# Last attention layer of a four-layer graph network: the weighted sum of values taken tile by tile with fp32 probabilities as the held operand, in place of fp16 halves summed over pairs of tiles

## Chip, cores, metric

One core of one Trainium2 chip. The metric is the device time of one execution in microseconds (us), median of the runs shown. TensorE does the matmuls, VectorE (DVE) and ScalarE (ACT) the work on rows, GpSimd (POOL) constants and some reductions, SyncE (SP) issues the transfers.

## What is computed

Four graph layers over 1250 nodes with 512 features, each behind a layer norm and a ReLU and each added to x. The change touches only the last one, cut here to what it computes:

```python
def _L3_gnn_ref(x, batch, ei, W):        # x is relu(layernorm(x)) of 1250 x 512
    scaling = float(64) ** (-0.5)
    q, k, v = jnp.split(x @ W, [512, 1024], axis=-1)
    q = (q * scaling).reshape(n, 8, 64)
    k = k.reshape(n, 8, 64)
    v = v.reshape(n, 8, 64)
    aw = jnp.einsum('ehf,ehf->eh', q[src], k[dest])
    m = jax.ops.segment_max(aw, src, num_segments=n)
    e = jnp.exp(aw - m[src])
    denom = jax.ops.segment_sum(e, src, num_segments=n)
    alpha = e / denom[src]
    out = jax.ops.segment_sum(alpha[:, :, None] * v[dest], src, num_segments=n)
    return out.reshape(n, 512)
```

There are 20000 edges, 8 heads of 64 features. The kernel holds the edges as a dense 1250 x 1250 table of counts, so a repeated edge is a count above one, and its logarithm is added to the score.

## The kernel before, in words

The nodes are 10 tiles of 125 rows. Per engine there is one hand-written program (`block.tensor`, `block.scalar`, `block.vector`, `block.sync`, `block.gpsimd`); the order of the work on an engine is the order in which its loops issue it, and semaphores tie the engines together. `after(eng, name, n)` is a wait for a count.

**Values.** In the last layer, per tile of nodes, TensorE makes v in 12 fp16 matmuls of 512 columns (L1826) into `psW[t % 2]`. ACT (L822) writes the upper half of v, scaled, as fp16 into `v_pair[.., t, h, 0, :]`; DVE (L1323) writes v minus that half as fp16 into `v_pair[.., t, h, 1, :]`. Around these stand, on the same two engines, the norm of a later tile (L802), the upper and lower halves of the turned h (L808, L1310) and of the weights (L632, L1250). `project_half` then makes k and q (L62), and `projected_up` and `projected_low` split these (L829, L1331).

**The loop.** Then 80 steps of a pipeline follow, one for each head h and tile t of targets (n = 10h + t). On TensorE step n issues, in this order: `turn_tile(n-2)`, 10 fp32 transposes (L1385) of the 125 x 1250 row of probabilities into `psW[1]`; a first part of the weighted sum; `score(n+1)`, 6 fp16 matmuls (L62) into `psW[0]`; the rest of the weighted sum; and in every second step `fold_pair`.

- DVE adds the logarithm of the counts to the scores and takes the row maximum (L1368), makes the negative maximum (L1371), and later, per four tiles, `add_quad` (L1352, L1353, L1358) divides and adds the four results to x.
- ACT takes the exponential with its row sum (L856), into `row3[n % 3]`.
- The turned probabilities (source on the partitions, target along the free dimension) leave PSUM twice: ACT (`upper`, L841 for blocks 0 to 7 and L843 for blocks 8 and 9) writes fp16 upper halves of 2^15 times the value, DVE (`lower`, L1344, L1346) the fp16 rest. `turned_a` and `turned_b` are these two pieces of `psW[1]`. The next tile's transposes wait for DVE's pieces (`lo3a`, `lo3b`).
- `weigh_pair` (L1879) works on two tiles of targets at once, spread over two steps (5 blocks in each, as 3 and 2 round the score): per block of 125 sources it holds v's two halves side by side (125 x 128 fp16) and streams first the two tiles' upper halves, then their lower halves (250 columns each), all 20 into one 128 x 250 result. ACT copies that result to `o_sum` (L545, 128 x 250). `fold_pair` (L1892) turns it back per tile and adds the two halves of v with a constant 128 x 64 matrix `fold`, made by POOL at the start.

```python
for j in blocks:
    for part in range(2):
        m = pe.matmul(small[:, 0:2 * ROWS], v_pair[0:ROWS, j, h, :, :].rearrange("p c d -> p (c d)"),
                      turned[pair % 2][0:ROWS, j, 2 * part:2 * part + 2, :].rearrange("p c i -> p (c i)"), ...)
```

## Time and profile before

| | us |
|---|---|
| median of 3 runs | 1238.27 |
| lowest, highest | 1237.48, 1239.95 |
| the profiled execution, its own time | 1239.9 |
| span of the profiled execution | 1238.2 |
| TensorE matmul busy in the span | 1132.0 |
| VectorE busy | 914.5 |
| ScalarE busy | 716.0 |

The trace lists weight loads (PEld) and matmuls (PE) of TensorE apart; the two overlap, and matmuls are pipelined, so the recorded duration of one matmul is longer than the distance to the next. The distance from one load to the next, or from one group's first load to the next group's first, is what a group of matmuls takes out of TensorE's time. A fp32 matmul that is no transpose is two records in the trace, a load and a matmul each. The last layer's loop of 80 steps runs from about 913 us to 1232 us of the span; the values are made from 832 us to 865 us. PEclk is the granted clock of TensorE as a share of the full one.

### The profile page before, as it was taken

The page shows a single profiled execution, that of the slowest core. Times are in us where ns is not written, and L with a number is a line of the kernel's source. Part 1 is how long each engine was busy: PE and PEld are TensorE (multiplying, and loading weights), DVE is VectorE, ACT ScalarE, POOL GpSimd, SP SyncE. Part 2 cuts the span into 40 slices and gives each one's busy share as a digit, 9 for nine tenths or more (in the row PEclk, how much of TensorE's full clock was granted, in tenths as well). Part 3 has the DMA queues.
Part 4 walks back from the last instruction along what each step waited for, and adds up shares of the span by engine and source line. Part 5 has one row for each costly group of instructions (what it writes and reads, how often), then busy time and mean ns, then how long its engine had stood idle before and what let it go on. Part 6 is the DMA issues. An engine that isn't in the chain of part 4 may idle for free. (4 is left out here: it accounts for less than half of the span.)

```text
span 1238.2 us, 16225 instructions
## 1 busy us (share of the span) xinstructions
PE 1132.0 (91%) x5959; PEld 714.8 (58%) x5959; DVE 914.5 (74%) x1652; ACT 716.0 (58%) x901; POOL 64.5 (5%) x117
## 2 busy tenths in 40 slices
PE   6999969996999977979999999969999999999996
PEld 4666635555785544434444444436557777777775
DVE  5999962017656697878899997865448888888885
ACT  2324846005548666058877877845137777777774
POOL 3000132000002100000000000000000000000000
PEclk9899989998999987979999999989999999999999
DMA  4000000003003000204111100000021001111002
GB/s 157 5 1 1 1 2 2 1 0 136 1 1 95 1 1 1 85 24 147 45 45 44 45 24 2 2 1 1 1 52 27 20 8 27 27 27 27 2 1 83
DMA packets 24771, 36.18 MB, mean 29 GB/s; under 512 B 11874, under 2 KB 13204, under 8 KB 24694
## 3 DMA queue, kind: packets, MB, share of 16 engines
q1 hardware_dynamic: 24694, 35.14, 9.4%
q8 instruction: 50, 0.82, 0.3%
q14 instruction: 27, 0.22, 0.1%
HBM read 26.03 MB, written 2.70 MB: 23 GB/s over the span
## 5 line engine op out<-in xcount | busy, mean ns | idle before, releaser
L62 PE MATMUL wide<-arena 125*125 125x512 bf16 (+5 forms) x2076 | 462.2, 372 | 16.3 <-DVE arena L962 7.5
L62 PEld LDWEIGHTS wide<-arena 125*125 125x125 bf16 (+5 forms) x2076 | 253.9, 131 | 197.9 <-issue 80.7
L1783 PE MATMUL wide<-arena 125*65 125x512 f32 (+1 forms) x480 | 182.3, 516 | 0.0
L1385 PE MATMUL wide<-ident,arena 125*125 125x125 f32 (+3 forms) x954 | 132.0, 286 | 11.6 <-ACT arena L618 4.2
L758 ACT ACTIVATE arena<-arena,b 125x1250 f32<-125x1250 f32 x80 | 106.7, 1336 | 60.1 <-PE wide L1783 55.8
L1278 DVE TENSOR_TENSOR arena<-wide,arena 125x1250 f32<-125x1250 f32 x80 | 116.7, 1459 | 31.2 <-PE wide L1773 31.1
L1385 PEld LDWEIGHTS wide<-ident,arena 125*125 125x125 f32 (+3 forms) x954 | 116.5, 187 | 21.8 <-issue 8.9
L841 ACT ACTIVATE arena<-wide 125x1000 f16<-125x1000 f32 x80 | 80.8, 1010 | 79.7 <-PE wide L1385 79.7
L1783 PEld LDWEIGHTS wide<-arena 125*65 125x65 f32 x480 | 63.4, 138 | 101.8 <-issue 95.4
L1344 DVE SCALAR_TENSOR_TENSOR arena<-wide,arena 125x1000 f16<-125x1000 f32 x80 | 95.9, 1199 | 33.6 <-ACT arena L841 33.6
L856 ACT ACTIVATE arena<-arena,neg_max,unit 125x1250 f32<-125x1250 f32 x80 | 114.3, 1429 | 5.7 <-DVE neg_max L1371 5.7
L1219 DVE CUSTOM_DVE_ANT_0 arena<-arena,cnt 125x1250 bf16<-125x1250 f32 x80 | 116.2, 1452 | 1.5 <-DVE b_max L1219 1.5
L1879 PE MATMUL small<-arena 125*128 125x250 f16 x800 | 112.7, 271 | 1.4 <-DVE arena L1346 1.4
L790 ACT ACTIVATE arena<-arena,b 125x1250 f32<-125x1250 f32 x80 | 106.0, 1325 | 8.4 <-DVE arena L1278 8.4
L961 DVE TENSOR_SCALAR arena<-arena 125x1250 bf16<-125x1250 f16 x180 | 98.4, 546 | 8.2 <-issue 7.3
L1385 PE MATMUL small<-ident,arena 125*125 125x125 f32 (+6 forms) x360 | 61.6, 314 | 44.3 <-ACT arena L575 15.3
L545 ACT ACTIVATE arena<-cntT 125x1250 f16<-125x1250 int16 x64 | 75.7, 1235 | 25.7 <-PE wide L62 25.4
L1879 PEld LDWEIGHTS small<-arena 125*128 125x128 f16 x800 | 72.1, 98 | 27.8 <-issue 20.2
L1385 PEld LDWEIGHTS small<-ident,arena 125*125 125x125 f32 (+6 forms) x360 | 52.9, 208 | 52.7 <-issue 18.6
L545 ACT ACTIVATE arena<-wide 65x512 f32<-65x512 f32 (+4 forms) x50 | 29.9, 640 | 76.4 <-PE wide L1453 50.1
L1771 PE MATMUL wide<-arena,sel_w 128*125 128x512 bf16 (+1 forms) x240 | 59.4, 357 | 15.5 <-DVE arena L1278 12.1
L990 DVE BATCH_NORM_STATS2 bns<-arena 128x6 f32<-128x512 f32 (+1 forms) x36 | 18.7, 581 | 62.7 <-ACT arena L673 62.6
(255 smaller groups left out, 1260.1 us busy)
## 6 DMA issues: line engine op xcount, KB each, us to landing
arena<-rows_kept SPq DMA_DIRECT2D x16, 625.0 KB, 5.9
arena<-arena SPq DMA_DIRECT2D x40, 156.2 KB, 2.9
arena<-in_L_gnn_W SPq DMA_DIRECT2D x3, 1024.0 KB, 7.7
x_nm<-in_x SPq DMA_DIRECT2D x2, 1250.0 KB
out<-x_nm SPq DMA_DIRECT2D x1, 2187.5 KB
arena<-in_L_gnn_W_l SPq DMA_DIRECT2D x1, 1024.0 KB, 6.3
arena<-in_L_gnn_W_r SPq DMA_DIRECT2D x1, 1024.0 KB, 8.4
arena<-in_L_gnn_Wk SPq DMA_DIRECT2D x1, 1024.0 KB, 5.3
```

Of the source, the lines that this page charges most:

```text
L62: mm = pe.matmul(ps[0:rows, lo:hi], lhsT, rhs[:, lo:hi], start=start, stop=stop, skip_group_check=True)
L545: return act.activation(dst, src, ACT.Copy, **k)
L758: act.activation(ring[n % RINGS][0:ROWS, :], t_bc[h % 2][0:ROWS, :], ACT.Relu, scale=0.8, bias=b08[0:ROWS, h, t:t + 1]).then_inc(S["relu2_ ...
L790: act.activation(row, row, ACT.Exp, bias=b02[0:ROWS, h, t:t + 1]).then_inc(S["exp2_made"], 1)
L856: act.activation(row, row, ACT.Exp, bias=neg_max[0:ROWS, n % TILES:n % TILES + 1], scale=unit[0:ROWS, 0:1], accum_out=den3[0:ROWS, n:n + 1 ...
L961: ts(hot_src[0:ROWS, g, :], iota_h[0:ROWS, :], e_col[0:ROWS, 1, c + g, :], None, ALU.is_equal)
L1219: dve.tensor_tensor_reduce(junk[0:ROWS, :], b_bc[h % 2][0:ROWS, :], mask[0:ROWS, i, :], 1.0, 2 * NEG, ALU.subtract, ALU.max, b_max[0:ROWS, ...
L1278: tt(row, psW[0][0:ROWS, 0:N], row, ALU.add).then_inc(S["z2_made"], 1)
L1344: stt(wide(2 + s), turned_a, UP, wide(s), ALU.mult, ALU.subtract).then_inc(S["lo3a"], 1)
L1385: return pe.transpose(dst, src, ident[0:k, 0:k])
L1783: m = pe.matmul(psW[1][0:VA, lo:hi], v_gat[0:ROWS, t, h, :], ring[n % RINGS][0:ROWS, lo:hi], start=(t == 0), stop=(t == TILES - 1))
L1879: m = pe.matmul(small[:, 0:2 * ROWS], v_pair[0:ROWS, j, h, :, :].rearrange("p c d -> p (c d)"), turned[pair % 2][0:ROWS, j, 2 * part:2 * p ...
```

## The change

The probabilities stay fp32. `turned` is now four buffers of 125 x 1250 fp32, one for each tile. ACT copies blocks 0 to 7 (`turned_out`), DVE blocks 8 and 9 (`turned_rest`), with no second pass and no factor 2^15. v is kept as fp32 `v_last`, written by DVE alone. `weigh(n, blocks)` holds a block of turned probabilities (125 sources x 125 targets, fp32) and streams v of that block (64 columns, fp32), so that the result of 10 matmuls is already the 125 x 64 of one tile, in the place in `small` where `add_quad` reads. `fold`, `o_sum`, `weigh_pair` and `fold_pair` are gone; the weighted sum runs three steps behind the score's step, 6 blocks ahead of the score and 4 behind it.

```diff
-        v_pair = region(16384, [TILES, H, 2, DH], F16)
+        v_last = region(16384, [TILES, H, DH])
-        o_sum = [region(13870 + 250 * i, [2 * ROWS]) for i in range(2)]
-        turned = [region(5120 + 2500 * i, [TILES, 4, ROWS], F16) for i in range(2)]
+        turned = [region(5120 + 1250 * i, [TILES, ROWS]) for i in range(QUAD)]
...
-            done(pool.memset(fold[:, :], 0.0))
-            for r in range(2):
-                done(pool.affine_select(out=fold[:, :], in_=fold[:, :], compare_op=ALU.not_equal, fill=1.0, base=-r * DH,
-                                        pattern=[[-1, DH]], channel_multiplier=1))
...
-                    act.wait_ge(S["v3_full"], t + 1)
-                    act.activation(v_pair[0:ROWS, t, :, 0, :], psW[t % 2][0:ROWS, 0:512].rearrange("p (h d) -> p h d", h=H), ACT.Copy,
-                                   scale=SCALED).then_inc(S["v3_hi"], 1)
...
+                def turned_out(n):
+
                     act.wait_ge(S["turned3a"], n + 1)
-                    if s == 0:
-                        after(act, "pv3_full", pair - 1)
-                    act.mul(dst[:, 0:8, :].rearrange("p (b c) i -> p b c i", b=2), turned_a, UP).then_inc(S["hi3a"], 1)
-                    act.wait_ge(S["turned3b"], n + 1)
-                    act.mul(dst[:, 8:10, :], turned_b, UP).then_inc(S["hi3b"], 1)
-
-                for n in range(H * TILES + 5):
-                    if n >= 6 and n % 2 == 0:
-                        pair = (n - 6) // 2
-                        act.wait_ge(S["pv3_full"], pair + 1)
-                        after(act, "folded3", pair - 1)
-                        copy(o_sum[pair % 2], small[:, 0:2 * ROWS]).then_inc(S["o3_out"], 1)
-                    if 2 <= n < H * TILES + 2:
-                        upper(n - 2)
+                    after(act, "pv3_full", n - QUAD + 1)
+                    copy(turned[n % QUAD][0:ROWS, 0:8, :].rearrange("p (b c) i -> p b c i", b=2), turned_a).then_inc(S["turned3a_out"], 1)
+
+                for n in range(H * TILES + 2):
+                    if n >= 2:
+                        turned_out(n - 2)
...
-                    dve.wait_ge(S["v3_hi"], t + 1)
-                    stt(v_pair[0:ROWS, t, :, 1, :], psW[t % 2][0:ROWS, 0:512].rearrange("p (h d) -> p h d", h=H), SCALED,
-                        v_pair[0:ROWS, t, :, 0, :], ALU.mult, ALU.subtract).then_inc(S["v3_out"], 1)
+                    dve.wait_ge(S["v3_full"], t + 1)
+                    ts(v_last[0:ROWS, t, :, :], psW[t % 2][0:ROWS, 0:512].rearrange("p (h d) -> p h d", h=H), SCALED, None,
+                       ALU.mult).then_inc(S["v3_out"], 1)
...
+                def turned_rest(n):
+
+                    dve.wait_ge(S["turned3b"], n + 1)
+                    after(dve, "pv3_full", n - QUAD + 1)
+                    dve.tensor_copy(turned[n % QUAD][0:ROWS, 8:10, :], turned_b).then_inc(S["turned3b_out"], 1)
...
-                    if n >= 9 and (n - 9) % QUAD == 0 and (n - 9) // QUAD < H * TILES // QUAD - 1:
-                        add_quad((n - 9) // QUAD)
-                    if 2 <= n < H * TILES + 2:
-                        lower(n - 2)
+                    if n >= 8 and n % QUAD == 0 and n // QUAD - 2 < H * TILES // QUAD - 1:
+                        add_quad(n // QUAD - 2)
+                    if n >= 2:
+                        turned_rest(n - 2)
...
+                def weigh(n, blocks):
+
+                    q, h = n // QUAD, n // TILES
                     if blocks[0] == 0:
-                        pe.wait_ge(S["lo3b"], 2 * pair + 2)
-                        after(pe, "o3_out", pair)
+                        pe.wait_ge(S["turned3a_out"], n + 1)
+                        after(pe, "acc_read", H + q - 1 if q >= 2 else 0)
+                    at = 512 * (q % 2) + DH * (n % QUAD)
                     for j in blocks:
-                        for part in range(2):
-                            m = pe.matmul(small[:, 0:2 * ROWS], v_pair[0:ROWS, j, h, :, :].rearrange("p c d -> p (c d)"),
-                                          turned[pair % 2][0:ROWS, j, 2 * part:2 * part + 2, :].rearrange("p c i -> p (c i)"),
-                                          start=(j == 0 and part == 0), stop=(j == TILES - 1 and part == 1))
+                        if j == 8:
+                            pe.wait_ge(S["turned3b_out"], n + 1)
+                        m = pe.matmul(small[0:ROWS, at:at + DH], turned[n % QUAD][0:ROWS, j, :], v_last[0:ROWS, j, h, :],
+                                      start=(j == 0), stop=(j == TILES - 1))
...
-                for n in range(H * TILES + 5):
+                for n in range(H * TILES + 3):
...
+                    if n >= 3:
+                        weigh(n - 3, range(6))
                     if n + 1 < H * TILES:
                         score(n + 1)
-                    if 4 <= n < H * TILES + 4:
-                        weigh_pair((n - 4) // 2, (range(5 * half + 3, 5 * half + 5)))
-                    if n >= 6 and n % 2 == 0:
-                        fold_pair((n - 6) // 2)
+                    if n >= 3:
+                        weigh(n - 3, range(6, TILES))
```

TensorE's own order in one step of the loop, before (out<-in, rows x columns; L1892 the fold, L1385 the transposes, L1879 the weighted sum, L62 the score):

```order
L1892 MATMUL small<-fold,arena 125x64 [waits acc_read,o3_out]
L1892 MATMUL small<-fold,arena 125x64
L1385 MATMUL wide<-ident,arena 125x125 [waits lo3a,exp3_made]
L1385 MATMUL wide<-ident,arena 125x125 x7
L1385 MATMUL wide<-ident,arena 125x125 [waits lo3b]
L1385 MATMUL wide<-ident,arena 125x125
L1879 MATMUL small<-arena 128x250 x6
L62 MATMUL wide<-arena 125x512 [waits score3_read]
```

And now (L1361 the transposes, L1857 the weighted sum, L61 the score):

```order
L1361 MATMUL wide<-ident,arena 125x125 [waits turned3a_out,exp3_made]
L1361 MATMUL wide<-ident,arena 125x125 x7
L1361 MATMUL wide<-ident,arena 125x125 [waits turned3b_out]
L1361 MATMUL wide<-ident,arena 125x125
L1857 MATMUL small<-arena 125x64 [waits acc_read,turned3a_out]
L1857 MATMUL small<-arena 125x64 x5
L61 MATMUL wide<-arena 125x512 [waits score3_read]
```

The fold is gone; the six matmuls ahead of the score hold 125 targets and stream 64 columns where they streamed 250; the transposes wait for a copy by ACT where they waited for DVE's second half.

DVE's order in one step, before (L1368 the sum with its maximum, L1344 and L1346 the lower halves):

```order
L1368 ISA arena,mcol<-wide,cnt 125x1250 [waits score3_full,turned3b]
L1368 ISA mcol 125x1
L1371 TENSOR_SCALAR neg_max<-mcol,unit 125x1 [waits score3_read]
L1352 TENSOR_SCALAR den<-den,unit 125x4 [waits folded3]
L1353 RECIPROCAL den<-den 125x4 [waits dve_done]
L1358 SCALAR_TENSOR_TENSOR x_nm<-small,den,x_nm 125x64 [waits dve_done]
L1358 SCALAR_TENSOR_TENSOR x_nm<-small,den,x_nm 125x64 x3
L1344 SCALAR_TENSOR_TENSOR arena<-wide,arena 125x8x125 [waits hi3a]
L1346 SCALAR_TENSOR_TENSOR arena<-wide,arena 125x2x125 [waits hi3b]
```

And now:

```order
L1344 ISA arena,mcol<-wide,cntT 125x1250 [waits score3_full,turned3b]
L1344 ISA mcol 125x1
L1347 TENSOR_SCALAR neg_max<-mcol,unit 125x1 [waits score3_read]
L1328 TENSOR_SCALAR den<-den,unit 125x4 [waits pv3_full]
L1329 RECIPROCAL den<-den 125x4 [waits dve_done]
L1334 SCALAR_TENSOR_TENSOR x_nm<-small,den,x_nm 125x64 [waits dve_done]
L1334 SCALAR_TENSOR_TENSOR x_nm<-small,den,x_nm 125x64 x3
L1322 COPY arena<-wide 125x250 [waits pv3_full,turned3b]
```

The pass over 125 x 8 x 125 behind the four-tile sum has left DVE; a copy of 125 x 250 remains.

## Rows read from the trace of the kernel before

**Rows 1.** The page's busy line, and the loop by windows (busy us, PEclk, DMA)

```profile
PE 1132.0 (91%) x5959; PEld 714.8 (58%) x5959; DVE 914.5 (74%) x1652; ACT 716.0 (58%) x901; POOL 64.5 (5%) x117
...
945.00:1222.00 277.00, 272.38 (x2030) 210.44 (x2029) 243.74 (x469) 205.53 (x328) 0.00 (x0) 1.00 0.10 23
```

**Rows 2.** The chain of waits from 900 us on: shares by line, two recurring pieces

```profile
by line: PE wide L1385 27.1%; PE wide L62 26.8%; PE small L1879 20.7%; ACT arena L856 7.5%; PE small L1892 4.5%; issue 3.9%; ACT arena L841 3.0%; ACT arena L843 2.0%; DVE arena L1344 1.4%; DVE arena L1368 0.4%; DVE arena L1331 0.4%; DVE x_n
...
951.29 1.41 ACT arena L856 x2
...
1195.83 1.41 ACT arena L856 x2
```

**Rows 3.** Timeline of TensorE's loads in one step: start, us, engine, line, operation

```profile
1002.10 0.52 PEld L1892 LDWEIGHTS small<-fold,arena 128*125 128x125 f32 x4
1002.53 1.17 PEld L1385 LDWEIGHTS wide<-ident,arena 125*125 125x125 f32 x10
1003.62 0.64 PEld L1879 LDWEIGHTS small<-arena 125*128 125x128 f16 x6
1004.27 0.46 PEld L62 LDWEIGHTS wide<-arena 128*125 128x125 f16 x3
...
1005.68 0.33 PEld L1879 LDWEIGHTS small<-arena 125*128 125x128 f16 x4 [0.27 <-issue]
1006.06 1.17 PEld L1385 LDWEIGHTS wide<-ident,arena 125*125 125x125 f32 x10
```

**Rows 4.** Timeline round the wait that recurs every fourth tile

```profile
1211.28 1.19 DVE L1344 SCALAR_TENSOR_TENSOR arena<-wide,arena 125x1000 f16<-125x1000 f32 x1
...
1212.59 1.17 PEld L1385 LDWEIGHTS wide<-ident,arena 125*125 125x125 f32 x10 [0.45 <-ACT arena L856]
```

**Rows 5.** fp32 matmuls of 65 columns in layer two: loads, and the stretch's windows

```profile
347.47 3.65 PEld L1600 LDWEIGHTS wide<-arena 128*128 128x128 f32 x32
...
347.50:350.80 3.30, 3.30 (x33) 3.30 (x31) 1.32 (x4) 2.79 (x6) 0.00 (x0) 1.00 0.00 0
```

**Rows 6.** Groups of the last layer by form: busy us, mean ns of one

```profile
L1879 PEld LDWEIGHTS small<-arena 125*128 125x128 f16 x800 | 72.1, 98 | 27.8 <-issue 20.2 <-DVE arena L1346 1.6
...
L1892 PEld LDWEIGHTS small<-fold,arena 128*125 128x125 f32 x160 | 20.6, 188 | 1.2 <-ACT arena L545 0.7
...
L1344 DVE SCALAR_TENSOR_TENSOR arena<-wide,arena 125x1000 f16<-125x1000 f32 x80 | 95.9, 1199 | 33.6 <-ACT arena L841 33.6
...
L841 ACT ACTIVATE arena<-wide 125x1000 f16<-125x1000 f32 x80 | 80.8, 1010 | 79.7 <-PE wide L1385 79.7
...
L1346 DVE SCALAR_TENSOR_TENSOR arena<-wide,arena 125x250 f16<-125x250 f32 x80 | 32.7, 409 | 0.0
```

**Rows 7.** Timeline of the transposes' loads: tiles 0, 1 and 2, and tile 77

```profile
922.78 1.79 PEld L1385 LDWEIGHTS wide<-ident,arena 125*125 125x125 f32 x10 [0.53 <-DVE arena L1331]
924.45 0.44 PEld L62 LDWEIGHTS wide<-arena 128*125 128x125 f16 x2
...
926.88 1.17 PEld L1385 LDWEIGHTS wide<-ident,arena 125*125 125x125 f32 x10 [0.34 <-issue]
...
930.41 0.73 PEld L1385 LDWEIGHTS wide<-ident,arena 125*125 125x125 f32 x6 [0.63 <-issue]
...
1216.50 1.17 PEld L1385 LDWEIGHTS wide<-ident,arena 125*125 125x125 f32 x10
```

**Rows 8.** Timeline of the end: the last fold and the last sum

```profile
1230.56 0.51 PEld L1892 LDWEIGHTS small<-fold,arena 128*125 128x125 f32 x4 [0.75 <-ACT arena L545]
...
1231.25 0.23 DVE L1352 TENSOR_SCALAR den<-den,unit 125x4 f32<-125x4 f32 x1 [3.94 <-PE small L1892]
```

**Rows 9.** Waits from 836 us to 866 us, where the values are made

```profile
PEld wide L1826 <- DVE arena L1310: 1.5, 4, 0.4
```

**Rows 10.** Windows over the first transposes and the score behind them

```profile
922.80:924.40 1.60, 1.60 (x9) 1.60 (x10) 1.56 (x3) 0.12 (x2) 0.00 (x0) 0.63 0.00 0
924.50:926.80 2.30, 2.30 (x8) 1.13 (x7) 1.27 (x2) 2.30 (x3) 0.00 (x0) 0.54 0.00 0
```

More of the change, by code:

```diff
@@ L45 @@
 ROWS3 = 3
-UP = 2.0 ** 15
 TOP16 = 2.0 ** 14
@@ L146, in gnn_program @@
         den3 = sb("den3", [128, H * TILES])
-        fold = sb("fold", [128, DH])
         w_most = sb("w_most", [128, 3])
@@ L1336, in _ @@
                         scaled_logs(t).then_inc(S["log_set"], 1)
-                def lower(n):
-                    dst = turned[n // 2 % 2][0:ROWS, :, :, :]
-                    s = n % 2
-                    wide = lambda i: dst[:, 0:8, i, :].rearrange("p (b c) i -> p b c i", b=2)
-                    dve.wait_ge(S["hi3a"], n + 1)
-                    stt(wide(2 + s), turned_a, UP, wide(s), ALU.mult, ALU.subtract).then_inc(S["lo3a"], 1)
-                    dve.wait_ge(S["hi3b"], n + 1)
-                    stt(dst[:, 8:10, 2 + s, :], turned_b, UP, dst[:, 8:10, s, :], ALU.mult, ALU.subtract).then_inc(S["lo3b"], 1)
+                def turned_rest(n):
+                    dve.wait_ge(S["turned3b"], n + 1)
+                    after(dve, "pv3_full", n - QUAD + 1)
+                    dve.tensor_copy(turned[n % QUAD][0:ROWS, 8:10, :], turned_b).then_inc(S["turned3b_out"], 1)
                 def add_quad(q):
-                    dve.wait_ge(S["folded3"], 2 * q + 2)
+                    dve.wait_ge(S["pv3_full"], QUAD * (q + 1))
                     rd = den3[0:ROWS, QUAD * q:QUAD * q + QUAD]
@@ L1861, in turn_tile @@
                     pe.wait_ge(S["exp3_made"], n + 1)
-                    after(pe, "lo3a", n)
+                    after(pe, "turned3a_out", n)
                     for j in range(8):
@@ L1865, in turn_tile @@
                     m.then_inc(S["turned3a"], 1)
-                    after(pe, "lo3b", n)
+                    after(pe, "turned3b_out", n)
                     for j in range(8, TILES):
@@ L1869, in turn_tile @@
                     m.then_inc(S["turned3b"], 1)
-                def weigh_pair(pair, blocks):
-                    h = 2 * pair // TILES
+                def weigh(n, blocks):
+                    q, h = n // QUAD, n // TILES
                     if blocks[0] == 0:
-                        pe.wait_ge(S["lo3b"], 2 * pair + 2)
-                        after(pe, "o3_out", pair)
+                        pe.wait_ge(S["turned3a_out"], n + 1)
+                        after(pe, "acc_read", H + q - 1 if q >= 2 else 0)
+                    at = 512 * (q % 2) + DH * (n % QUAD)
                     for j in blocks:
-                        for part in range(2):
-                            m = pe.matmul(small[:, 0:2 * ROWS], v_pair[0:ROWS, j, h, :, :].rearrange("p c d -> p (c d)"),
-                                          turned[pair % 2][0:ROWS, j, 2 * part:2 * part + 2, :].rearrange("p c i -> p (c i)"),
-                                          start=(j == 0 and part == 0), stop=(j == TILES - 1 and part == 1))
+                        if j == 8:
+                            pe.wait_ge(S["turned3b_out"], n + 1)
+                        m = pe.matmul(small[0:ROWS, at:at + DH], turned[n % QUAD][0:ROWS, j, :], v_last[0:ROWS, j, h, :],
+                                      start=(j == 0), stop=(j == TILES - 1))
                     if blocks[-1] == TILES - 1:
                         m.then_inc(S["pv3_full"], 1)
-                def fold_pair(pair):
-                    pe.wait_ge(S["o3_out"], pair + 1)
-                    q = pair // 2
-                    after(pe, "acc_read", H + q - 1 if q >= 2 else 0)
-                    for s in range(2):
-                        at = 512 + DH * (QUAD * (q % 2) + 2 * (pair % 2) + s)
-                        m = pe.matmul(small[0:ROWS, at:at + DH], o_sum[pair % 2][:, s * ROWS:(s + 1) * ROWS], fold[:, :], start=True, stop=True)
-                    m.then_inc(S["folded3"], 1)
                 pe.wait_ge(S["proj3_out"], 2 * KD - 1)
@@ L1904, in _ @@
                         turn_tile(n - 2)
-                    half = n % 2
-                    if 4 <= n < H * TILES + 4:
-                        weigh_pair((n - 4) // 2, (range(5 * half, 5 * half + 3)))
+                    if n >= 3:
+                        weigh(n - 3, range(6))
                     if n + 1 < H * TILES:
                         score(n + 1)
-                    if 4 <= n < H * TILES + 4:
-                        weigh_pair((n - 4) // 2, (range(5 * half + 3, 5 * half + 5)))
-                    if n >= 6 and n % 2 == 0:
-                        fold_pair((n - 6) // 2)
+                    if n >= 3:
+                        weigh(n - 3, range(6, TILES))
             phase_end(pe, 3)
```

11 lines of the change are left out of this document (4 added, 7 removed).

## Prediction

> **What bounds the kernel now.** I read the page's busy line first, then the windows, the chain of waits, and the timeline of one step. TensorE is busy 91% of the span, and 272.4 of 277 us inside the loop, where its granted clock is the full one (1.00, so 2.4 GHz); DVE has 243.7 and ACT 205.5 us there [rows 1]. Busy alone proves little for pipelined matmuls, so the chain matters: from 900 us on, 79% of it is TensorE's own work (the lines 1385, 62, 1879 and 1892), and the one piece that recurs with another engine stands 16 x 4 tiles apart from 951.29 to 1195.83 us, 15.28 us for four tiles, or 3.82 us a tile [rows 2]. The timeline shows why: TensorE's groups stand end to end [rows 3]. From first load to first load, ten transposes take 1.09 us (1002.53 to 1003.62), six matmuls of the weighted sum 0.65, the score 1.41, the other four 0.38: 3.53 us. The fold adds 0.43 us in every second step, 0.215 a tile. That is 3.745 of 3.82; the rest is one wait in four tiles. There the load of the transposes stood idle 0.45 us before 1212.59 [rows 4]. The row names ACT's L856, but the transposes of that tile wait for DVE's lower half of the tile before, which ended at 1211.28 + 1.19 = 1212.47, late because the sum of four tiles had stood ahead of it. So the last layer is bound by how fast TensorE gets through its loads and streams.
>
> **The weighted sum: the term that decides.** Removed per tile are ten fp16 records at 0.65 + 0.38 = 1.03 us, and 0.215 us of fold. Added are ten fp32 matmuls, each of which holds a 125 x 125 block and streams 64 columns. The nearest rows are two. The fold is of just this kind, with 125 held columns and 64 streamed; two calls are four records and took 0.43 us from load to load (1002.10 to 1002.53) [rows 3], 0.1075 a record. Layer two has 16 calls with 65 streamed columns as 32 records without a break: (3.65 - 0.19)/31 = 0.112 us a record, 0.19 being one load's recorded length, for 128 held columns [rows 5]. The transposes, again 125 held fp32 columns, have (1.17 - 0.19)/9 = 0.109 [rows 3]. I take 0.109 and two records a call: 20 x 0.109 = 2.18 us a tile. The streams of 64 columns are too short to cover a load; before, a load hid under 250 streamed columns, and that cover is what the change gives up. Halving the arithmetic (no lower halves) buys nothing, since records are what is paid: 20 loads a tile for 12 before.
>
> A step then is 1.09 + 2.18 + 1.41 = 4.68 us. The score's 1.41 holds some handover round its loads that load-bound neighbours could hide, about 0.06 by the same rows read from matmul to matmul, so I take **4.65 us** a tile, and 4.53 to 4.80 as ends: the low one with 0.1075 a record and 0.12 of handover hidden, the high one with layer two's 0.112 and 0.06 lost.
>
> By the Trainium skill, "TensorE: Matmul & The Clock Gate", section "LDWEIGHTS (loading the stationary operand)", a load costs its columns over 1.2 GHz, so 104 ns for 125; as an estimate from that page the 20 records would be 2.08 us and the forecast 7 us lower. The three rows above are longer, so they stand in the sum. The same page, section "Weight-path perf modes", gives a fast load to 128 columns of a type that is not FP32, which speaks against this change. The trace agrees in the recorded lengths, 98 ns for the old 128-column fp16 load and 188 ns for the fold's fp32 one [rows 6].
>
> **Who waits instead.** ACT's pass over the first eight blocks stays at about 1.01 us, its small pass (and the copy of the pair's sum) goes; DVE loses 1.20 us and turns 0.41 us into a copy that I bound by the same 0.41 [rows 6]. From 72.6 tiles in the window, DVE has 3.36 us a tile and ACT 2.83 [rows 1], so they fall to about 2.2 and 2.3 beside a step of 4.65. The next transposes need only ACT's copy, which begins 0.9 us into a step and ends about 2.1; that has 2.5 us of slack, and the wait of 0.07 us a tile goes. Queued behind DVE's wait for `turned3b` is only the next row maximum, whose score comes later in the step. With four buffers the copy waits for a weighted sum that ended two steps before. Nothing new is late. POOL's three instructions for `fold` are hidden: POOL is 5% busy [rows 1] and nobody waits for what follows them.
>
> **Start, end and values.** Transposes of tile 1 begin at 926.88 and of tile 2 at 930.41 [rows 7]; the weighted sum now begins one step earlier, so tile 2 begins 4.65 after tile 1, at 931.53: +1.1. Tile 77 began at 1216.50, 75 tiles after tile 2 at 3.815 each. Now 75 x (4.65 - 3.815) = +62.6. From tile 77 to DVE's last sum it took 1231.25 - 1216.50 = 14.75 us [rows 7, 8], with a chain through ACT and DVE in each step, then a sum, a copy and a fold. Now it is three steps without a score, 3 x (1.09 + 2.18) = 9.81, then 19 x 0.109 + 0.36 = 2.43, where 0.36 is what lay between the last load of the fold (1230.56 + 3 x 0.11) and DVE's start [rows 8]: 12.24, so -2.5. The last sum and the transfer of the result stay. In the values ACT no longer stops for v3, so the turned h comes earlier: TensorE's loads waited 1.5 us in four times for it [rows 9]; I take all of it, -1.5, and bound it by 0 from the other side. DVE's write of v stays one pass of about the same length.
>
> **Sum:** 1.1 + 62.6 - 2.5 - 1.5 = +59.7 us. Against the profiled execution (span 1238.2, its own time 1239.9) that is a span of 1297.9 and 1299.6 us. That execution lay 1.6 us above the median of 1238.27, so a median of **1298.0 us**, 4.8% slower. Per tile the ends 4.53 and 4.80 move it by -9.1 and +11.4.
>
> **The rivals.**
>
> *Loads hide under the score's wide streams* (0.05). Loads can run ahead of the matmuls, and the score leaves gaps between them, 0.27 us before 1005.68 [rows 3]. If every stream were hidden, 36 loads at 0.109 would be 3.92 us a tile: 0.4 + 75 x 0.105 - 2.5 - 1.5 = +4.3, 1242.6 us. Against it: the loads of a score never began in bulk while an earlier matmul streamed; they keep one ahead.
>
> *One record a call* (0.03), the one on the faster side. The transposes hold fp32 too and are one record each [rows 3]. If the weighted sum's calls were also one load and one stream, it would cost 1.09 us a tile, a step 3.59: 0.1 - 75 x 0.225 = -16.8, at the end about -6.5 (a step without a score is then bound by transposes and ACT's copy, some 2.3 us), -1.5 in the values: about 1213.5 us. It decides once a call costs under 0.14 us (then a step is under 3.87). Against it: the fold's two calls and layer two's 16 show two records each, and the fold differs in nothing but its held data [rows 3, 5].
>
> *TensorE's clock falls to its lower level, 1.2 GHz, for stretches of the loop* (0.04), since short streams and transposes now fill 70% of a step. At a granted 0.63 ten transposes took 1.67 us (922.78 to 924.45), at 0.54 a score 2.43 (to 926.88) [rows 7, 10], 0.58 and 1.02 more than at full clock, and 20 short records up to 1.16 more: 1.6 to 2.8 us a tile. In half of the tiles that is 60 to 110 us on top, about 1383 us. Against it: the clock stayed 1.00 where nothing but 65-column matmuls ran [rows 5]; TensorE had waited before the stretch at 0.54 and will not wait in this loop. The skill's same page, section "Part 4: PE-mode transpose", says that the fast clock does not engage for transposes; the window at 1.00 over the loop, with ten in each step, speaks against it here.
>
> *A wait that I missed* (0.03), say a copy late by 0.5 us in each step: 1338 us.
>
> **Chances and range.** The forecast has 0.85. A measurement of this kernel tells about 0.2%, 2.5 us, from no change. All cases but one are beyond that on the slow side: slower 0.96, same 0.01 (part of the hidden loads, with the ends saved), faster 0.03. The range holds the forecast's own ends with a little over, 1288 to 1310, and leaves the rivals out.
>
> **What would show it.** In the changed profile: 1600 records for the weighted sum; distances of 0.107 to 0.112 us between them; tile to tile 4.5 to 4.8 us with no wait of TensorE for `turned3a_out`; granted clock 1.00 from 945 us to the end of the loop; transposes of tile 77 near 1279 us; values about 1.5 us shorter; DVE and ACT under 60% busy there. The forecast falls if there are 800 records, if the loads stand closer than 0.10 us, or if the clock row shows less than 0.95.

## The result, and the profile after

The changed kernel takes 1295.53 us (median of 4 runs, 1294.09 to 1301.57) against 1238.78 us for the kernel before on the same chip: 1.0466 times as long, with a 95% interval of 1.0437 to 1.0496. The forecast was 1298.0 us, in a range from 1288 to 1310.

The profiled execution has a span of 1292.4 us and a time of 1294.1 us of its own. Its page, the busy line and the fp32 weighted sum (L1857), and the window of the loop (busy us of PE, PEld, DVE, ACT and POOL, PEclk, DMA):

```profile
PE 1192.5 (92%) x6599; PEld 792.3 (61%) x6599; DVE 832.3 (64%) x1572; ACT 676.4 (52%) x771; POOL 63.8 (5%) x114
...
L1857 PE MATMUL small<-arena 125*125 125x64 f32 x1600 | 199.7, 272 | 0.0
L1857 PEld LDWEIGHTS small<-arena 125*125 125x125 f32 x1600 | 186.6, 189 | 20.4 <-issue 20.4
...
945.00:1270.00 325.00, 325.00 (x2535) 275.98 (x2535) 167.46 (x392) 168.91 (x211) 0.00 (x0) 1.00 0.08 19
```

These answer to [rows 1]: 800 calls are 1600 records, TensorE is busy for all of the 325 us at full clock, and DVE and ACT are busy for 52% of them. TensorE's own lines are 97% of the chain of waits from 900 us on, where they were 79% before [rows 2]:

```profile
by line: PE small L1857 46.2%; PE wide L61 27.6%; PE wide L1361 23.6%; DVE arena L1344 0.4%; DVE arena L1311 0.4%; DVE x_nm L1334 0.2%; issue 0.1%; DVE den L1328 0.1%; DVE neg_max L1347 0.1%; DVEq L332 0.0%; DVE den L1329 0.0%; DVEq L850 0.
```

One step in the timeline of TensorE's loads (start, us, engine, line, operation), beside [rows 3]:

```profile
1004.19 0.95 PEld L1857 LDWEIGHTS small<-arena 125*125 125x125 f32 x8 [0.27 <-issue]
...
1005.06 1.17 PEld L1361 LDWEIGHTS wide<-ident,arena 125*125 125x125 f32 x10
...
1006.15 1.39 PEld L1857 LDWEIGHTS small<-arena 125*125 125x125 f32 x12
...
1007.46 0.41 PEld L61 LDWEIGHTS wide<-arena 128*125 128x125 f16 x3
...
1008.82 0.95 PEld L1857 LDWEIGHTS small<-arena 125*125 125x125 f32 x8 [0.27 <-issue]
```

From first load to first load: transposes 1.09 us as before, 12 records of the sum 1.31 (0.109 each), the score 1.36, 8 records 0.87. A step is 4.62 to 4.63 us. Before, each of the weighted sum's records took 0.109 us too (0.65 us for six), there beside streams of 250 columns; there were ten of them a tile, and two of the fold, where now there are 20.

The transposes' loads of tiles 0, 1 and 2 and of tile 77, and DVE's last sum, beside [rows 7, 8]:

```profile
917.76 1.92 PEld L1361 LDWEIGHTS wide<-ident,arena 125*125 125x125 f32 x10 [0.53 <-DVE arena L1311]
921.86 1.17 PEld L1361 LDWEIGHTS wide<-ident,arena 125*125 125x125 f32 x10 [0.27 <-issue]
926.48 1.17 PEld L1361 LDWEIGHTS wide<-ident,arena 125*125 125x125 f32 x10
...
1273.19 1.17 PEld L1361 LDWEIGHTS wide<-ident,arena 125*125 125x125 f32 x10
...
1285.45 0.23 DVE L1328 TENSOR_SCALAR den<-den,unit 125x4 f32<-125x4 f32 x1 [3.90 <-PE small L1857]
```

With these marks the two profiled executions can be laid side by side. Every term is the difference of two such distances:

| stretch | before, us | after, us | difference | forecast |
|---|---|---|---|---|
| start to the first turned h of the last layer | 829.6 | 827.1 | -2.5 | 0 |
| from there to the projections (the values) | 35.8 | 33.3 | -2.5 | -1.5 |
| projections to tile 0's transposes | 57.3 | 57.4 | 0.0 | 0 |
| tile 0 to tile 2 | 7.6 | 8.7 | +1.1 | +1.1 |
| tile 2 to tile 77, 75 steps | 286.1 | 346.7 | +60.6 | +62.6 |
| tile 77 to DVE's last sum | 14.75 | 12.26 | -2.5 | -2.5 |
| from there to the end | 6.95 | 6.95 | 0 | 0 |

### The profile page after: what moved, and what is told of

It is laid out like the page before. It is cut to its first block and busy times, and to the rows that moved or that the text cites. A ratio compares the mean times of both kernels' runs of the same rounds, so it can differ in the third digit from the quotient of the medians.

```text
span 1292.4 us, 17363 instructions
## 1 busy us (share of the span) xinstructions
PE 1192.5 (92%) x6599; PEld 792.3 (61%) x6599; DVE 832.3 (64%) x1572; ACT 676.4 (52%) x771; POOL 63.8 (5%) x114
## 5 line engine op out<-in xcount | busy, mean ns | idle before, releaser
L61 PE MATMUL wide<-arena 125*125 125x512 bf16 (+5 forms) x2076 | 457.7, 369 | 15.9 <-DVE arena L942 7.6
L61 PEld LDWEIGHTS wide<-arena 125*125 125x125 bf16 (+5 forms) x2076 | 248.9, 130 | 193.4 <-issue 76.6
L538 ACT ACTIVATE arena<-wide 125x1000 f32<-125x1000 f32 (+4 forms) x130 | 110.4, 864 | 250.5 <-PE wide L1361 196.1
L1857 PE MATMUL small<-arena 125*125 125x64 f32 x1600 | 199.7, 272 | 0.0
L1857 PEld LDWEIGHTS small<-arena 125*125 125x125 f32 x1600 | 186.6, 189 | 20.4 <-issue 20.4
L1361 PE MATMUL wide<-ident,arena 125*125 125x125 f32 (+3 forms) x954 | 131.8, 286 | 6.9 <-ACT arena L611 4.7
L1361 PEld LDWEIGHTS wide<-ident,arena 125*125 125x125 f32 (+3 forms) x954 | 116.5, 187 | 10.8 <-issue 6.4
L1344 DVE CUSTOM_DVE_ANT_0 arena<-wide,cnt 125x1250 f32<-125x1250 f32 x40 | 58.4, 1460 | 80.2 <-PE wide L61 80.2
L1361 PE MATMUL small<-ident,arena 125*125 125x125 f32 (+6 forms) x360 | 59.4, 306 | 45.6 <-ACT arena L568 15.7
L1344 DVE CUSTOM_DVE_ANT_0 arena<-wide,cntT 125x1250 f32<-125x1250 f32 x32 | 46.7, 1460 | 65.1 <-PE wide L61 65.1
L538 ACT ACTIVATE arena<-cntT 125x1250 f16<-125x1250 int16 x64 | 75.5, 1235 | 24.5 <-PE wide L61 24.1
L1361 PEld LDWEIGHTS small<-ident,arena 125*125 125x125 f32 (+6 forms) x360 | 50.7, 200 | 53.5 <-issue 18.2
L970 DVE BATCH_NORM_STATS2 bns<-arena 128x6 f32<-128x512 f32 (+1 forms) x36 | 18.7, 581 | 62.7 <-ACT arena L666 62.6
```

What stands on the lines that cost most here:

```text
L61: mm = pe.matmul(ps[0:rows, lo:hi], lhsT, rhs[:, lo:hi], start=start, stop=stop, skip_group_check=True)
L538: return act.activation(dst, src, ACT.Copy, **k)
L1344: dve.tensor_tensor_reduce(row3[n % ROWS3][0:ROWS, :], psW[0][0:ROWS, 0:N], log_tile(t)[0:ROWS, :], 1.0, LOWEST, ALU.add, ALU.max, mcol[0: ...
L1361: return pe.transpose(dst, src, ident[0:k, 0:k])
L1857: m = pe.matmul(small[0:ROWS, at:at + DH], turned[n % QUAD][0:ROWS, j, :], v_last[0:ROWS, j, h, :], start=(j == 0), stop=(j == TILES - 1))
```

## The experiments

### Does the load set a record, or the stream? (stream96, stream192)

```diff
-                        m = pe.matmul(small[0:ROWS, at:at + DH], turned[n % QUAD][0:ROWS, j, :], v_last[0:ROWS, j, h, :],
+                        wide = DH if h == H - 1 else 96
+                        v_flat = v_last[0:ROWS, j, :, :].rearrange("p h d -> p (h d)")
+                        m = pe.matmul(small[0:ROWS, at:at + wide], turned[n % QUAD][0:ROWS, j, :], v_flat[:, DH * h:DH * h + wide],
```

> The changed kernel, but each matmul of the weighted sum streams 96 columns of v (32 of the next head, written over by the next tile) in the first seven heads. Theory (a record costs its held block's load, 0.109 us, and the stream hides under the next load): 96 fp32 columns are 80 ns at two cycles each, still under the load, so the step stays at 4.62 us and the time at about 1295 us, within 3 us. Rival (the stream is paid on top of something fixed): 32 columns are 27 ns, 20 records, 70 tiles, so +37 us, about 1332 us.

Measured: 1298.95 us in one run. The loads of the weighted sum still stand 0.109 us apart. The step is 4.65 us where the changed kernel has 4.62, and the 0.03 us lie in the score's group (1.38 for 1.36), not in the sum's: 1.8 us from tile 2 to tile 77 (348.5 against 346.7), where the rival asked for 37. Most of the rest stands ahead of the loop (below). The second run is the same with `192` and heads 0 to 5.

> The changed kernel with 192 streamed columns of v in the first six heads (128 of them from the next two heads, written over). Theory of the load: 192 fp32 columns are 160 ns at two cycles each, now over the load, so a record becomes about 0.163 us; +0.054 x 20 = +1.07 us a tile over 60 tiles, about 1360 us. Rival (stream paid on top): 128 columns more are 107 ns, +128 us, about 1423 us.

Measured: 1361.33 us. Its loads in one step:

```profile
1041.15 1.27 PEld L1859 LDWEIGHTS small<-arena 125*125 125x125 f32 x8 [0.27 <-issue]
1042.40 1.22 PEld L1361 LDWEIGHTS wide<-ident,arena 125*125 125x125 f32 x10
1043.54 1.92 PEld L1859 LDWEIGHTS small<-arena 125*125 125x125 f32 x12
1045.44 0.14 PEld L61 LDWEIGHTS wide<-arena 128*125 128x125 f16 x1
```

12 records in 1.90 us are 0.158 us each, and most of them stand 0.163 apart, which fits 192 columns at two cycles of 2.4 GHz (0.160). So a fp32 record takes the longer of its stream and its load: 96 columns (0.080 by the same two cycles, an estimate) hide under the load of 0.109, 192 do not. The rival that adds the stream on top fell in both runs.

### Does the held width set the load? (hold64, hold32)

```diff
-                        m = pe.matmul(small[0:ROWS, at:at + DH], turned[n % QUAD][0:ROWS, j, :], v_last[0:ROWS, j, h, :],
+                        m = pe.matmul(small[0:DH, at:at + DH], turned[n % QUAD][0:ROWS, j, 0:DH], v_last[0:ROWS, j, h, :],
```

`add_quad` works on the same 64 rows.

> The changed kernel, but each matmul of the weighted sum holds 64 of the 125 targets, and only these rows are added to x: the other 61 targets of each tile are left out. Theory of the load: a held block of 64 columns loads in about half of the time, a record is 0.053 to 0.06 us, the weighted sum 1.1 to 1.2 us a tile, the step about 3.6 us, the time 1212 to 1222 us. Rival (a fp32 record costs 0.109 us whatever it holds, by its issue or its two passes): no change, 1295 us.

Measured: 1251.70 us in one run, between the two. Its loads in one step, and the page's line with the mean length of one load, 137 ns:

```profile
1041.58 0.54 PEld L1857 LDWEIGHTS small<-arena 125*64 125x64 f32 x8 [0.27 <-issue]
1042.19 1.17 PEld L1361 LDWEIGHTS wide<-ident,arena 125*125 125x125 f32 x10
1043.47 0.77 PEld L1857 LDWEIGHTS small<-arena 125*64 125x64 f32 x12
1044.32 0.41 PEld L61 LDWEIGHTS wide<-arena 128*125 128x125 f16 x3
...
L1857 PEld LDWEIGHTS small<-arena 125*64 125x64 f32 x1600 | 104.8, 137 | 29.8 <-issue 20.4
```

Within a group the loads stand (0.77 - 0.137)/11 = 0.058 us apart, where the changed kernel has 0.109. So the load does shrink with what is held, and the theory had the record right. What it missed stands between the groups. From the last load of one group to the first of the next it takes 0.21 us from the sum to the transposes, 0.31 from the transposes to the sum and 0.21 from the sum to the score; the changed kernel has 0.109 at each. Against the 0.058, 0.109 and 0.058 that the records alone would ask, that is 0.15 + 0.20 + 0.15 = 0.5 us a step, which is what separates the expected step of about 3.6 us from the measured 4.08. The transposes themselves keep their pace (1.17 us as before). In `split125` below, where all held blocks have 125 columns, the same three distances are 0.058, 0.109 and 0.058 in a step without waits, so the cost goes with passing between 64 and 125 held columns. Why it arises is not shown.

The same with 32 held targets:

> The changed kernel, holding only 32 of the 125 targets in each matmul of the weighted sum (the other 93 are left out). With 64 held the records stood 0.071 to 0.076 us apart, not 0.053 to 0.06, and the step was 4.09 us. Theory A (a load costs about 0.03 us and 0.62 ns a column, a line through 0.071 at 64 and 0.109 at 125): 32 columns load in 0.051, so the stream of 64 fp32 columns, 0.053 to 0.056, sets the record; the step falls by another 0.3 us or more, about 1228 us. Theory B (a record has a floor of about 0.07 us whatever it holds or streams): step stays at 4.0 to 4.1 us, 1247 to 1252 us.

Measured: 1241.93 us in one run, a step of 3.98 to 3.99 us. The 0.071 to 0.076 us from which the expectation starts are distances from group to group divided by the number of records, so they hold a share of these passages and are no price of a record. Between single loads it is 0.056 us here and 0.058 with 64 held, both near the 0.053 that 64 streamed fp32 columns take at two cycles each (an estimate from `stream192`), and the passages cost the same again (0.20, 0.31 and 0.20 us). So the record fits the stream, as theory A had it, but the 0.3 us that it promised from the mixed distance were not there to gain (0.1 us came); the floor of 0.07 us in theory B is not there, though its step (4.0) is the nearer one. The times of both were missed.

### Is it the 125 columns or the fp32? (split125, split128)

Both bring back fp16 halves of the probabilities and of v, but keep the new order on TensorE: the probabilities are held, upper half and then lower half, and v's two halves are streamed side by side. DVE's order is another one: its sum of four tiles, which has a copy and an addition more, stands behind the lower halves, where both kernels have it ahead.

```diff
-                        m = pe.matmul(small[0:ROWS, at:at + DH], turned[n % QUAD][0:ROWS, j, :], v_last[0:ROWS, j, h, :],
-                                      start=(j == 0), stop=(j == TILES - 1))
+                        held = 128 if j < 7 or j == 8 else ROWS
+                        for s in range(2):
+                            m = pe.matmul(small[0:held, at:at + 2 * DH], turned[n % QUAD][0:ROWS, s, ROWS * j:ROWS * j + held],
+                                          v_pair[0:ROWS, j, h, :, :].rearrange("p c d -> p (c d)"),
+                                          start=(j == 0 and s == 0), stop=(j == TILES - 1 and s == 1))
```

`split125` has `held = ROWS`. Per four tiles DVE adds the result's two halves before it adds to x.

> The changed kernel's order, with fp16 halves: the turned probabilities as upper and lower fp16 halves (ACT and DVE passes as before), each block held as 125 columns of fp16, twice, v's two fp16 halves streamed side by side (128 columns), and DVE adds the two halves of the result per four tiles. 20 records a tile of fp16 with 125 held columns. Theory (the held columns' load sets a record at 0.109 us in fp16 too, where it is 125 columns): step about 4.62 us, and the values as before, 1296 to 1301 us. Rival (the load of fp32 is slower than that of fp16): records of 0.056 us, step about 3.6 us, 1220 to 1235 us.

Measured: 1268.51 us in one run. Its loads in a step without waits:

```profile
1041.33 0.54 PEld L1877 LDWEIGHTS small<-arena 125*125 125x125 f16 x8 [0.27 <-issue]
1041.79 1.17 PEld L1379 LDWEIGHTS wide<-ident,arena 125*125 125x125 f32 x10
1042.88 0.82 PEld L1877 LDWEIGHTS small<-arena 125*125 125x125 f16 x12
1043.63 0.41 PEld L62 LDWEIGHTS wide<-arena 128*125 128x125 f16 x3
```

12 records of 125 held fp16 columns take 0.75 us, and single loads stand 0.058 apart, with twice as many streamed columns as the fp32 ones. My theory fell here: the price of 0.109 belongs to fp32, not to 125 columns. (One load is 0.14 us long in the trace and so overlaps the next ones.)

> As the run with fp16 halves and 125 held columns, but eight of the ten blocks hold 128 columns (three of the next block, whose output rows nobody reads). Theory from the recorded lengths (98 ns for a load of 128 fp16 columns, 137 for 125): a load of exactly 128 fp16 columns is the fast one; 16 of 20 records fall to 0.056 to 0.07 us, the weighted sum to 1.3 to 1.55 us, the step to 3.75 to 4.05 us, 1230 to 1255 us. Rival (128 columns load no faster, the recorded length is no price): 0.112 us a record, step about 4.65 us, 1298 to 1303 us.

Measured: 1270.53 us in one run. The loads once more:

```profile
1043.93 0.49 PEld L1877 LDWEIGHTS small<-arena 125*128 125x128 f16 x8 [0.27 <-issue]
1044.34 1.17 PEld L1379 LDWEIGHTS wide<-ident,arena 125*125 125x125 f32 x10
1045.43 0.77 PEld L1877 LDWEIGHTS small<-arena 125*128 125x128 f16 x12
1046.15 0.41 PEld L62 LDWEIGHTS wide<-arena 128*125 128x125 f16 x3
```

The groups take 0.72 and 0.41 us where they took 0.75 and 0.46, single loads stand 0.056 us apart for 0.058, and a step without waits is 3.57 us where `split125` has 3.65. The Trainium skill, "TensorE: Matmul & The Clock Gate", section "Weight-path perf modes", reserves the fast load for 128 columns of a type that is not FP32. Here 128 columns in 16 of 20 records are worth 0.08 us a step, while the recorded length of a load differs much more (98 ns for 138, medians). Both records stand near their stream's 0.053, so the run does not show what the fast load alone takes. Neither time was the expected one (1220 to 1235 us for the rival that `split125` bore out, 1230 to 1255 for `split128`), because such steps are only some of the loop: from tile 0's to tile 79's transposes it is 333.9 and 333.7 us, 4.22 us a step on average. The largest wait of `split128` between 945 and 1180 us says why:

```profile
PE wide L62 <- DVE mcol L1362: 22.6, 14, 1.7
```

Once in four steps TensorE waits up to 1.7 us for a row maximum, ahead of which DVE's whole sum of four tiles stands, and the step behind it is often late too: of four steps two take 3.6 us, one 5.4 to 5.8 and one 3.6 to 5.2. Spreading the sum, with a copy moved to ACT, took most of this away (below).

### The wait in every fourth tile of the kernel before (lower_first, pairs_spread)

```diff
-                    if n >= 9 and (n - 9) % QUAD == 0 and (n - 9) // QUAD < H * TILES // QUAD - 1:
-                        add_quad((n - 9) // QUAD)
                     if 2 <= n < H * TILES + 2:
                         lower(n - 2)
+                    if n >= 9 and (n - 9) % QUAD == 0 and (n - 9) // QUAD < H * TILES // QUAD - 1:
+                        add_quad((n - 9) // QUAD)
...
-                    after(pe, "acc_read", H + q - 1 if q >= 2 else 0)
+                    after(pe, "acc_read", H + q if q >= 1 else 0)
```

> The kernel before, with DVE's lower halves ahead of the sum of four tiles, and the fold of the next four waiting for that sum. Theory (the wait that recurs every fourth tile is for DVE's lower half, not for ACT's exponential that the row names): the 0.27 us in four tiles go, 20 of them, 5 us, 1234 us. Rival (it is the exponential, or the sum's delay moves to the fold): no change, 1239 us.

Measured: 1251.74 us, 1.0103 times the time before (1.0086 to 1.0120). The old wait is gone, and a longer one stands elsewhere (waits from 945 to 1180 us):

```profile
PEld wide L62 <- DVE mcol L1368: 17.3, 15, 1.2
```

That is 15 waits of about 1.15 us in 60 steps for the row maximum, which now runs behind the sum. So it was DVE's order that made the wait; ACT's exponential, which the row in [rows 4] names, was not it, since nothing of ACT was changed. The time is neither the theory's 1234 nor the rival's 1239 us: moving the sum cost more than it won. Spreading the sum over four steps was the next try:

```diff
+                    if n >= 9 and step == 0:
+                        take_quad(q)
                     if 2 <= n < H * TILES + 2:
                         lower(n - 2)
+                    if n >= 9 and step == 1:
+                        reciprocals(q)
+                        add_tiles(q, [0])
+                    if n >= 9 and step == 2:
+                        add_tiles(q, [1, 2])
+                    if n >= 9 and step == 3:
+                        add_tiles(q, [3])
```

> The kernel before, with DVE's sum of four tiles taken apart: one copy of 125 x 256 out of PSUM where the sum stood, ahead of the lower halves, and the reciprocals and the four additions spread over the next three steps behind the lower halves. Theory (the wait in every fourth tile is for DVE's lower half, which 1.26 us of sum delay): with 0.35 us ahead of it the wait goes, 5 us in 20 groups of four, about 1233.5 us. Rival (any work on DVE in that step ends up in front of the row maximum and so of the next score, as when the lower halves went first, which took 12 us more): 1239 us or more.

Measured: 1246.54 us, 1.0057 times (1.0041 to 1.0074), so the theory's 1233.5 us fell. The loop itself is as long as before, 300.8 us from tile 0's to tile 79's transposes: the 0.27 us in four tiles went, and waits of up to 0.2 us for the row maximum came. What is lost is lost at the end, where the larger output transfer left later, here first and in the kernel before second:

```profile
1220.70 12.07 SPq L465 DMA_DIRECT2D out<-x_nm  x2
```

```profile
1211.39 21.50 SPq L464 DMA_DIRECT2D out<-x_nm  x2
```

A group of four is now finished three steps later. The last sum ends at 1229.8 us and the span at 1243.9, 23.2 us behind the issue of that transfer; in the kernel before the span ends 5.6 us behind its last sum. From tile 79's transposes to the end it is 23.7 us against 14.6; the last layer began earlier in this execution (see the next section), so the spans lie 5.7 us apart.

### Values by ACT (v_by_act)

```diff
+                    act.wait_ge(S["v3_full"], t + 1)
+                    act.activation(v_last[0:ROWS, t, :, :], psW[t % 2][0:ROWS, 0:512].rearrange("p (h d) -> p h d", h=H), ACT.Copy,
+                                   scale=SCALED).then_inc(S["v3_out"], 1)
...
-                    dve.wait_ge(S["v3_full"], t + 1)
-                    ts(v_last[0:ROWS, t, :, :], psW[t % 2][0:ROWS, 0:512].rearrange("p (h d) -> p h d", h=H), SCALED, None,
-                       ALU.mult).then_inc(S["v3_out"], 1)
```

> The changed kernel, but ACT writes v in fp32 and DVE does not, so that ACT again stops for each tile's v. My step on the values: TensorE waits again for the turned h, about 1.5 us in the stretch from the first turned h to the projections, so 1297 us. Rival (the 2.5 us that this stretch lost came from the clock coming back sooner, not from ACT): the stretch stays at 33.3 us and the time at 1295.5 us.

Measured: 1299.81 us (4 runs), where the theory had 1297 and the rival 1295.5. The stretch from the first turned h to the projections is 35.85 us long, as in the kernel before, and the wait of [rows 9] is back to the digit:

```profile
PEld wide L1802 <- DVE arena L1293: 1.5, 4, 0.4
```

In `stream96`, where ACT does not stop, it is 34.4 us; in the profiled execution of the changed kernel 33.3. So ACT's stops are worth 1.4 us, and the last 1.1 us are the clock, as the first value's 12 matmuls show, in the changed kernel and, second, in `v_by_act` (`stream96` and the kernel before have 5.35 too):

```profile
829.72 4.26 PE L1802 MATMUL wide<-arena 128*125 128x512 f16 x12 [0.70 <-DVE arena L1290]
```

```profile
832.79 5.35 PE L1802 MATMUL wide<-arena 128*125 128x512 f16 x12 [0.70 <-DVE arena L1293]
```

TensorE had waited 8 us before, and the clock stood at the lower level (PEclk 0.50 from 826 to 834 us in the kernel before, which is 1.2 GHz); in one execution it came back before these matmuls were done, in the others after. That belongs to no part of the change: `pairs_spread`, which makes its values as the kernel before does, has 4.23 us there. The clock differs in the same way at tile 0: its transposes and the score behind them take 4.10 us in both kernels (granted 0.57 in the changed one), and 2.87 us in `stream96` at 1.00. Nor does the start of the last layer, at 827.0 to 830.2 us in all these profiles, follow the kernels, although little ahead of it differs (POOL's three instructions for `fold`, the places of buffers). In `v_by_act` it is 3.1 us later than in the changed kernel, and with the 2.5 us of the stretch that makes the 5.6 us by which the two spans differ.

### A version that beats both (split128_spread, split128_out3)

`split128_spread` is `split128` with DVE's sum over four steps; ACT copies one half of the result and a semaphore of its own frees the bank.

```diff
+                    if n >= 8 and step == 0:
+                        reciprocals(q)
+                    if n >= 8 and step == 1:
+                        halves_added(q)
+                        add_tiles(q, [0])
+                    if n >= 8 and step == 2:
+                        add_tiles(q, [1, 2])
+                    if n >= 8 and step == 3:
+                        add_tiles(q, [3])
```

> The run with fp16 halves and 128 held columns, with DVE's work for four tiles spread over four steps and ACT copying one half of the result. Theory (there the records stood 0.052 to 0.060 us apart and three of four steps took 3.57 us; only the fourth was lengthened by up to 1.7 us, because DVE's whole sum stood ahead of the row maximum): the step is 3.57 to 3.65 us throughout, the time 1220 to 1226 us, less than both kernels. Rival (DVE's 3.3 us of work a tile, with its waits for ACT, sets the step): 3.75 us and more, 1233 us or above.

Measured: 1238.73 us, 0.9996 times the time before (0.9981 to 1.0012): no difference, and not the theory's 1220 to 1226 us. Yet the loop is shorter, 294.2 us from tile 0's to tile 79's transposes against 300.8. That is 3.72 us a step on average, between theory and rival, and three of four steps take 3.6 to 3.7 us, the fourth 4.0. From 945 us on DVE is busy for 219.7 of 235 us and TensorE for 231.2. TensorE's loads still wait 4.7 us there for the row maximum, in 12 of some 63 steps; that DVE's work sets the length of the step fits this, but no run tested it.

```profile
945.00:1180.00 235.00, 231.15 (x2268) 182.35 (x2265) 219.66 (x425) 174.75 (x269) 0.00 (x0) 1.00 0.10 22
```

The gain was lost at the end. The last sum and the two transfers of the output in its timeline:

```profile
1214.31 12.06 SPq L472 DMA_DIRECT2D out<-x_nm  x2
...
1223.30 0.87 DVE L1369 SCALAR_TENSOR_TENSOR x_nm<-arena,den,x_nm 125x64 f32<-125x64 f32 x4
```

The computation is over at 1224.2 us, the span at 1237.5. The transfer of 448 of 512 columns was issued only 9.9 us before the last sum's end, and the span ends 23.2 us behind that issue, as in `pairs_spread`. (In the kernel before, 1211.39 + 23.2 is 1234.6 us, ahead of the span's end at 1238.2.) So the output was cut in three:

```diff
-            for n, part in ((18, slice(0, D - DH)), (20, slice(D - DH, D))):
+            for n, part in ((10, slice(0, D // 2)), (18, slice(D // 2, D - DH)), (20, slice(D - DH, D))):
```

> The run with fp16 halves, 128 held columns and spread sums, with the output stored in three parts: columns of heads 0 to 3 once ten groups of four tiles are added, heads 4 to 6 after 18, head 7 at the end. There the last sum ended at 1224.2 us, 8.4 us before that of the kernel before, but the span ended 13.3 us later, and the large transfer had been issued at 1214.3. Theory (the 448-column transfer, 2.2 MB, now ends last): with four heads stored early the end is the last sum and 5.6 us, about 1230 us of span and 1231.5 us. Rival (something else holds the end, or the transfer in the loop slows the loop): 1236 us or more.

Measured: 1230.17 us, 0.9921 times the time before (0.9907 to 0.9935), as expected. The span ends 5.5 us behind the last sum:

```profile
1222.31 0.87 DVE L1369 SCALAR_TENSOR_TENSOR x_nm<-arena,den,x_nm 125x64 f32<-125x64 f32 x4
1223.21 0.26 SPq L472 DMA_DIRECT2D out<-x_nm  x1
```

The control has the three parts and nothing else:

> The kernel before with the output stored in the same three parts and nothing else. Theory: there the last sum ends at 1232.6 us, 21 us after the large transfer was issued, so the transfer hardly holds the end: 1236 to 1239 us, at most 2 us gained. Rival (what is gained above is the output's parts alone): 1231 to 1233 us here too.

Measured: 1239.44 us, 0.9999 times (0.9986 to 1.0012). The three parts alone gain nothing; they free the 8.8 us that the shorter loop (6.6) and the shorter way from tile 79's transposes to the last sum (6.8 us for 9.0) had made. The spans of the two profiled executions differ by 9.5.

## Why the prediction was right, and where it was not

**The bound.** TensorE's end-to-end groups were the bound, and still are: no wait of TensorE for another engine shows from 945 to 1270 us. The old wait of 0.07 us a tile went, as said, and `lower_first` bears out that it was for DVE's lower half and not for the exponential.

**The weighted sum.** The step was forecast at 4.65 us and measured at 4.623, from 20 records of 0.109 us. The nearest row, the fold of the same held and streamed widths in the same type [rows 3], gave the price to within 2%; the remaining 2 us of the 62.6 are the handover round the score, of which 0.05 us are hidden (1.36 us where the loads showed 1.41) and the forecast had taken 0.03. `stream96` and `stream192` confirm that the load was the longer of the two, and `hold64` that it shortens with the held columns (0.058 us for 64).

**The reason behind that price was half wrong.** The prediction said that halving the arithmetic buys nothing since records are what is paid, 20 loads a tile for 12. `split125` has 20 records as well, with the same 125 held columns, and pays 0.058 us for each: the weighted sum 1.2 us a tile, not 2.2. What is paid is the fp32 held block. The number was right because its rows were fp32 rows, not because of the count. The rule of the Trainium skill, "TensorE: Matmul & The Clock Gate", section "LDWEIGHTS (loading the stationary operand)", gives 104 ns for 125 columns, near the fp32 load's 0.109 us; the fp16 loads of the same 125 columns do not follow it, they stand 0.058 us apart.

**Start, end, values.** The start of the loop (+1.1) and the end (-2.5) came out as worked out. The values' gain of 1.5 us was the right one for its cause (`v_by_act` against `stream96`: 35.85 and 34.43 us, 1.4 us). The profiled execution gained 1.1 us more there by the clock and 2.5 us in stages that the change does not touch; neither was forecast, and both vary from one execution to the next. With the 2.0 us of the loop these make the 5.5 us by which the span fell short of the forecast's 1297.9.

**The rivals.** None decided. Loads hidden under the score's streams: the distance from load to load stayed at 0.109, and only the handover was hidden. One record a call: 800 calls are 1600 records. The clock: 1.00 from 945 to 1270 us, with ten transposes in each step, which stand 0.109 us apart. That speaks against the sentence of the Trainium skill, same page, section "Part 4: PE-mode transpose", that the fast clock does not engage for them; but they are only 1.09 of 4.62 us here, so a stretch of transposes alone stays untested. A missed wait: none.

## What to carry to other kernels

When a matmul streams few columns, cost it by the distance between records of the same held type: a fp32 held block of 125 columns took 0.109 us here, the same block as a fp16 half 0.058, so two fp16 records for the two halves cost about as much as one fp32 record, and a fp32 matmul is two. Look for such a row before a sum is moved to the short-stream side. Take that distance within one group, the recorded stretch less one load over the number of loads less one, and read the passage to the next group apart: `hold64` seemed to have a floor of 0.07 us a record only because the two were mixed. And when a loop gets shorter and the time does not, look at the last transfer: 6.6 us won in the loop were invisible until the output left in three parts.

## What had not been expected of the hardware

- A fp16 load of 125 columns repeats every 0.058 us, a fp32 one every 0.109, although their recorded lengths (138 and 189 ns, medians) differ far less.
- Fp32 records with 64 or 32 held columns stand 0.058 and 0.056 us apart, but three passages a step between them and the 125-column blocks cost 0.15 to 0.20 us each beyond the records' own distance, 0.5 us a step; the fourth, behind the score, costs nothing. With 125 columns throughout there is no such cost. The cause is open.
- Moving 1.26 us of DVE work behind a pass of 1.6 us cost 12.7 us in the loop of `lower_first` (313.5 us from tile 0's to tile 79's transposes against 300.8), where its old place had cost about 5 (0.27 us in each of 20 groups, an estimate).
- In `pairs_spread` and in `split128_spread` the span ends 23.2 us behind the issue of the output transfer of 448 columns (2187 KB), and 13 to 14 us behind the last sum.
